# Two key tiles in one visit of the value products, with sixteen homes for the exponentials

## The reference

```python
kv = (mem @ W_kv).reshape(B, Nkv, 2, HEADS, HEAD_DIM)      # mem = ctx_1024, 16 heads of 16
q = (x @ W_q).reshape(B, Nq, HEADS, HEAD_DIM)              # x = layernorm(x)
attn = softmax(einsum('bhqd,bhkd->bhqk', q, k) * SCALE)
out = einsum('bhqk,bhkd->bhqd', attn, v)
x = x + tanh(g_xattn) * (out @ W_proj + b_proj)
# then x = x + tanh(g_ffn) * ffn(layernorm(x)):
# a router picks 2 of 8 experts (silu(g) * u @ w_down, hidden 384) for each token,
# and a shared expert is added for all
```

## Time and profile before

| what | value |
|---|---|
| median of 3 runs | 493.08 us |
| the profiled execution | 493.61 us |
| its span | 491.9 us |
| TensorE, VectorE, ScalarE busy | 97%, 62%, 53% of the span |
| TensorE's granted clock | full up to the last of the 40 slices |

### The profile page before, as it was taken

How to read it: one execution, slowest core, us unless ns; L and a number is a source line. 1 busy time by engine, 2 the same in 40 slices (tenths; PEclk the granted TensorE clock), 3 DMA queues, 4 the chain that set the end, 5 groups by cost and what they waited for, 6 DMA issues and landing times.

```text
span 491.9 us, 7745 instructions
## 1 busy us (share of the span) xinstructions
PE 476.5 (97%) x2783; PEld 286.3 (58%) x2783; DVE 305.9 (62%) x574; ACT 261.0 (53%) x416; POOL 183.9 (37%) x216
## 2 busy tenths in 40 slices
PE   8999999999999999999989999999999999999992
PEld 7665523333233233334446465699799799799992
DVE  3666779999899999996464699533333333333331
ACT  1665277777777777776544400306346346244430
POOL 4810178872231111111000023604547647767332
PEclk9999999999999999999999999999999999999997
DMA  7733408866753565211104001322334525445232
GB/s 246 236 102 105 138 7 228 218 182 183 212 147 87 159 165 163 65 34 55 33 24 149 1 2 43 113 93 46 63 53 65 76 45 87 65 63 78 33 33 32
DMA packets 36741, 48.30 MB, mean 98 GB/s; under 512 B 6240, under 2 KB 29920, under 8 KB 36704
## 3 DMA queue, kind: packets, MB, share of 16 engines
q1 hardware_dynamic: 21536, 26.16, 18.8%
q0 software_dynamic: 7344, 9.84, 13.1%
q10 hardware_dynamic: 7824, 11.81, 7.6%
HBM read 30.16 MB, written 14.29 MB: 90 GB/s over the span
## 4 chain that ended last, share of the span: by engine, by line
PE 94%; DVE 3%; ACT 1%; issue 1%; POOLq 0%; POOL 0%
PE ps L1284 73%; PE ps L1370 13%; PE ps L1646 2%; PE ps L1657 2%; PE ps L1290 1%; PE ps L1679 1%; DVE rows L894 1%; DVE neg_max L929 1%; ACT ctx_region L763 1%; PE ps L1300 1%; PE ps L1362 0%; PE ps L1518 0%; PE ps L1527 0%; POOLq L143 0%; DVE stats L880 0%
## 5 line engine op out<-in xcount | busy, mean ns | idle before, releaser
L763 ACT ACTIVATE ctx_region<-ps 128x512 f32<-128x512 f32 x256 | 140.7, 594 | 47.5 <-PE ps L1284 47.5
L929 DVE TENSOR_REDUCE neg_max<-ps 128x2 f32<-128x1024 f32 x128 | 151.0, 1209 | 21.5 <-PE ps L1284 19.6
L1284 PE MATMUL ps<-unit_region 96*128 96x512 bf16 (+1 forms) x512 | 128.4, 380 | 1.2 <-ACT ctx_region L763 0.7
L1284 PEld LDWEIGHTS ps<-unit_region 96*128 96x128 bf16 (+1 forms) x512 | 45.0, 97 | 101.4 <-ACT ctx_region L763 45.2
L1284 PE MATMUL ps<-unit_region,ctx_region 128*128 128x128 f32 (+1 forms) x824 | 97.4, 274 | 0.0
L1284 PEld LDWEIGHTS ps<-unit_region,ctx_region 128*128 128x128 f32 (+1 forms) x824 | 94.3, 188 | 0.7 <-DVE x_sb L1071 0.3
L655 POOL DMA_INDIRECT out<-unit_region x39 | 61.2, 1570 | 54.2 <-DMA out<-unit_region 31.0
L1284 PE MATMUL ps<-dn_region,unit_region 128*128 (+1 forms) x294 | 70.0, 381 | 0.0
L844 ACT COPY ctx_region<-up_region 128x1536 f32 x33 | 48.5, 1472 | 34.8 <-PE ps L1284 27.2
L1241 DVE TENSOR_TENSOR unit_region<-unit_region,ps 128x384 f32<-128x384 f32 x35 | 19.4, 555 | 71.5 <-ACT unit_region L861 62.6
L1284 PEld LDWEIGHTS ps<-dn_region,unit_region 128*128 128x128 f32 x294 | 53.2, 190 | 8.4 <-issue 2.8
(11 more groups left out here) (200 smaller groups left out, 464.8 us busy)
## 6 DMA issues: line engine op xcount, KB each, us to landing
up_region<-in_w_upT ACTq DMA_DIRECT2D x9, 768.0 KB, 4.5
qk_parts<-up_region SPq DMA_DIRECT2D x24, 192.0 KB, 3.2
unit_region<-qk_parts SPq DMA_DIRECT2D x24, 192.0 KB, 4.1
dn_region<-in_w_downT ACTq DMA_DIRECT2D x9, 384.0 KB, 5.3
unit_region<-up_region SPq DMA_DIRECT2D x48, 64.0 KB, 2.6
unit_region<-qk_parts SPq DMA_DIRECT2D x24, 128.0 KB, 4.1
ctx_region<-in_ctxT SPq DMA_DIRECT2D x4, 512.0 KB, 10.4
x_rows<-rows SPq DMA_DIRECT2D x4, 512.0 KB, 3.9
```

What stands on the lines that cost most here:

```text
L763: nc.scalar.activation(probs[:, k % 8, :], bank(SCORE_HOME[u, k]), ACT.Exp).then_inc(exp_done, 1)
L929: nc.vector.tensor_reduce(neg_max[:, s, 2 * p:2 * p + 2], bank(2 * (p % 2), 2), AX.X, ALU.max, negate=True).then_inc(max_done, 1)
L1284: return nc.tensor.matmul(o_, w, m, start=start, stop=stop)
```

## The change

In units 6 to 13 the visits are made for two key tiles at a time. Key tiles 0 and 1 are visited together behind s9, and key tiles 2 and 3 together behind s1 of the next unit. A visit waits for the exponentials of both of its tiles. Since twice as many exponentials stand at once, those of k = 8 to 15 get eight more homes in xnT, where whole q and k stood until GpSimd had split them (split_done). The waits of ScalarE for free homes are counted anew in visits_ahead.

```diff
@@ -129,6 +129,8 @@
 VALUES = 5
 PAIRS = TOPK * NT
 TABLE_PARTS = 4
+PV_BY_TWO = range(6, 14)
+PROBS = 8
 OUT_ROWS = N + 2 * P
 
 
@@ -154,6 +156,12 @@
         ctx_region = sb("ctx_region", [P, DC * N])
         ctx_sb = ctx_region[:, :].rearrange("p (c n) -> p c n", c=DC)
         probs = ctx_region[:, :].rearrange("p (s n) -> p s n", n=T)
+        probs_beyond = xnT[:, :, :].rearrange("p c n -> p (c n)").rearrange("p (s n) -> p s n", n=T)
+
+        def probs_home(u, k):
+
+            return probs_beyond[:, k - PROBS, :] if u in PV_BY_TWO and k >= PROBS else probs[:, k % PROBS, :]
+
         up_now = ctx_region[:, 0:2 * DC * FFN].rearrange("p (s c f) -> p s c f", s=2, c=DC)
         up_region = sb("up_region", [P, (E + 1) * DC * FFN])
         w_up = up_region[:, :].rearrange("p (e c f) -> p e c f", e=E + 1, c=DC)
@@ -754,13 +762,24 @@
                 act.wait_ge(nmT_ps, u + 1)
                 nc.scalar.copy(nmT[:, :], bank(SCORE_HOME[u - 1, TURNED])[0:HG * TB, 0:P]).then_inc(nmT_sb, 1)
 
+            def visits_ahead(u, kt):
+
+                two, two_ahead = u in PV_BY_TWO, u - 1 in PV_BY_TWO
+                if kt < 2 and two_ahead:
+                    return (u - 1) * TB + 2
+                if kt >= 2 and two:
+                    return u * TB if two_ahead else 0
+                return u * TB + kt - 1
+
             def exp_slot(u, g, first=False, more_max=True):
                 for k in range(TB * HG):
                     kt = k // HG
-                    if k % HG == 0 and not (first and kt < 2):
-                        act.wait_ge(pv_done, u * TB + kt - 1)
+                    if k % HG == 0 and visits_ahead(u, kt) > 0:
+                        act.wait_ge(pv_done, visits_ahead(u, kt))
+                    if u in PV_BY_TWO and k == PROBS:
+                        act.wait_ge(split_done, len(SPLIT_ORDER))
                     act.wait_ge(score_ps, u * TB * HG + k + 1)
-                    nc.scalar.activation(probs[:, k % 8, :], bank(SCORE_HOME[u, k]), ACT.Exp).then_inc(exp_done, 1)
+                    nc.scalar.activation(probs_home(u, k), bank(SCORE_HOME[u, k]), ACT.Exp).then_inc(exp_done, 1)
                     if k == 4 and more_max:
                         copy_max(u + 1)
 
@@ -1363,12 +1382,12 @@
                                     ident[:, :]).then_inc(nmT_ps, 1)
 
             def pv(u, s, kt, first=False):
-                pe.wait_ge(exp_done, u * TB * HG + kt * HG + HG)
+                pe.wait_ge(exp_done, u * TB * HG + (kt | 1 if u in PV_BY_TWO else kt) * HG + HG)
                 if kt == 0 and not first:
                     pe.wait_ge(o_done, u)
                 for h in range(HG):
                     last = nc.tensor.matmul(bank(6)[h * VW:(h + 1) * VW, :], v_home(u // NG)[:, kt, u % NG * HG + h, :],
-                                            probs[:, (kt * HG + h) % 8, :], start=kt == 0, stop=kt == TB - 1,
+                                            probs_home(u, kt * HG + h), start=kt == 0, stop=kt == TB - 1,
                                             skip_group_check=True)
                 last.then_inc(pv_done, 1)
 
@@ -1394,8 +1413,13 @@
                     mm(bank(SCORE_HOME[u, k]), k_unit[0:KROWS + MROWS, s, h, kt * P:(kt + 1) * P],
                        q_unit[0:KROWS + MROWS, s, h, :]).then_inc(score_ps, 1)
                     if k == 1 and not first:
-                        pv(u - 1, (r - 1) % NG, TB - 1)
-                    if kt >= 1 and h == 1:
+                        for last_kt in range(TB - 2 if u - 1 in PV_BY_TWO else TB - 1, TB):
+                            pv(u - 1, (r - 1) % NG, last_kt)
+                    if u in PV_BY_TWO:
+                        if kt == 2 and h == 1:
+                            pv(u, s, 0)
+                            pv(u, s, 1)
+                    elif kt >= 1 and h == 1:
                         pv(u, s, kt - 1, first)
                     if more_max and h == HG - 1:
                         for i in range(2):
```

## The result

The changed kernel takes 503.14 us (median of 4 runs, 502.71 to 503.52), the kernel before 493.07 us in the same comparison: ratio 1.0201, 95% interval [1.0183, 1.0219]. That is 10.1 us slower, where 10.8 us were forecast. The profiled execution took 503.15 us, its span is 501.4 us.

What follows compares the result with a forecast made beforehand. TensorE was taken to bound units 6 to 13. Per unit, - 2 x 0.19 + 0.84 + 0.48 + 0.40 = + 1.34 us; over eight units + 10.8, so 493.08 + 10.8 = 503.9 us, range 496.5 to 507.5.

Steps and rivals of the forecast that it cites:

- What bounds the stretch: Units 6 to 13: TensorE, busy 91.63 of 92 us, bounds them, and its readers have little time to spare.
- the walk: One unit of the new order followed by the old trace's steps: 6.41 + 6.34 = 12.75 us.
- The three waits: TensorE held each unit: s6 for the maxima copy 0.84 us, s15 for an exponential 0.48, m14 for a reduction 0.40.
- 2.00 us, 0.19 less than two apart: Cost of a merged visit on TensorE with 0.45 us between passes; 16 merges save 3.0 us.
- The 0.64 of the other bound: Rival: the step between merged visits costs 0.64 us, nothing saved, 506.9 us; within the 0.85 for all three waits.
- No wait at m6: First half: the second reduction is free at 3.54 us, m6 comes at 3.55, only because s6 has waited.
- Edits at no cost: New homes, ScalarE's waits, weight loads in the merged visit, take_out and SyncE's operand loads add no time.
- Everything behind unit 13 is shifted as a whole: After the changed units, the rest of the kernel only moves later, as TensorE has the chain there too.
- The full gain: Rival: readers keep ahead, TensorE is not held, merges save 3.0 us, 490.1 us; chance 0.05.
- Only the wait of s6: Rival: both second-half waits are covered, + 3.7 us, 496.8 us; chance 0.07.
- The clock: Rival: granted clock falls from 2.4 to 1.2 GHz in these units, up to 85 us more, 578 us; chance 0.02.
- The profile's signs: Units 12.7 to 12.8 us, three waits, passes 0.45 us apart, VectorE idle over 1 us, TensorE busy 87%, clock 1.00.

Runs made afterwards that it cites:

- e2: The changed kernel with only key tiles 0 and 1 visited together, 2 and 3 one at a time behind s13 and s1; 498.4 us, ratio 1.0101.
- e3: The changed kernel with only key tiles 2 and 3 visited together, 0 and 1 one at a time behind s5 and s9; 498.15 us, ratio 1.0102.
- e5: The changed kernel with the copy of the transposed maxima behind the exponential of k = 3, not k = 4, in units 6 to 13; 502.97 us.
- e7: The changed kernel with the copy behind the exponential of k = 3 and reductions over half of the keys in units 6 to 13; 496.78 us.
- e4: The changed kernel with the two visits of each pair pushed apart by one score; 506.87 us, ratio 1.0277.
- e8: The kernel before, with VectorE's reductions over half of the keys in units 6 to 13; 492.72 us against 493.38, ratio 0.9989.
- e1: The changed kernel without its merges, keeping the sixteen homes and ScalarE's new waits; 493.25 us against 492.95, ratio 1.0007.
- e10: The changed kernel with half-key reductions, visits reordered behind s1 and s10, copy behind the exponential of k = 3; 490.11 us, ratio 0.9941.
- e6: The changed kernel with VectorE's reductions over half of the keys in units 6 to 13; 499.02 us, ratio 1.0114.
- e9: The changed kernel reordered, both merges kept: visits behind s0 and m7, copy behind the exponential of k = 3, full reductions; 500.52 us, ratio 1.0151.
- e12: The kernel of e9 with each visit waiting only for its own key tile's exponentials; 495.41 us, ratio 1.0042.
- e11: The kernel of e10 with its order kept but reductions over all keys; 506.04 us, ratio 1.0269.

## Why the prediction was right, point by point

- **What bounds the stretch.** Right. TensorE had no slack there, so every wait and every saving came out nearly one to one: the old unit 11.45 us, the new one 12.73, forecast 12.75 by the walk.
- **The three waits.** Right in place, cause and size. Start to start in the changed kernel, s15 at 166.07 was due at 163.63 + 9 x 0.217 = 165.58, 0.49 us held (0.48 forecast); m14 at 167.12 comes 3.49 us behind s10 (3.48). s6 at 172.63 comes 2.69 us behind s2 at 169.94 (2.68), where 1.84 was due, 0.85 us held (0.84). e2 and e3 show each wait with its half, e5 to e7 which engine causes which.
- **The term that was mis-sized** is "2.00 us, 0.19 less than two apart". The first pass of a visit is 0.45 us, each later one 0.43: 0.31 - 0.22 + 0.45 + 0.43 + 0.43 + 0.55 = 1.95 us, so a merge saves 0.24. e4 measured 0.23. Over 16 merges this is 16 x 0.05 = 0.8 us. The 0.64 of the other bound falls, and with it that rival. The measured 0.43 agrees with what the Trainium skill (TensorEngine Tiling (Array Packing), Tiling Modes, Key Properties) says, that only a change of the tiling mode drains the engine.
- **Where the 10.8 and the 10.1 us part.** The 0.8 us above are near the difference of 0.7, but they are not its account. With them alone the new unit would be 12.65 us, and it is 12.73. Small terms went the other way: m6 is held 0.03 us, the second matmul behind each wait comes 0.01 us later than usual, and the old unit is 11.45 us where its steps give 11.43. That the walk met the unit within 0.02 us is in this part luck. In the traces seven units grow by 1.28 to 1.32 us, 0.3 to 0.4 us less in all than the sum has. The eighth, from the transpose in unit 13 to that in unit 14, goes from 11.31 to 12.30 us, 0.99 more, as the wait of 0.30 us of unit 14 goes (see e8). That gives 10.05 us.
- **No wait at m6 "only because s6 has waited"**: right but for 0.03 us, and e5 is the proof, as the wait appears there.
- **Edits at no cost**: right for the homes and ScalarE's waits (e1). "Everything behind unit 13 is shifted as a whole" is off by the 0.30 us of unit 14. The weight loads stand ahead of the merged visit (166.55 and 166.97 us) and not in it, at no cost: the exponential of k = 15 is done at 3.85, as forecast.
- **Rivals.** The full gain needs fast readers and another order (e10). Only the wait of s6: the second half's waits were both there. The clock: the granted clock stayed 1.00, 2.4 GHz, with TensorE busy 83.50 of 92 us. What the Trainium skill (TensorE: Matmul & The Clock Gate, A second HAM failure mode: psum-queue depth-cycling) tells of short idle times between groups of matmuls did not come about in this kernel.
- **The profile's signs.** All as listed but three. The later passes of a merged visit are 0.43 us apart and not 0.45. VectorE idles 0.75 us ahead of the fifth reduction in units with the transpose back; over 1 us was said, which left that transpose out; the longest such wait, in a unit without it, is 1.4 us. The busy share was 91%, not 87%, as the view counts a matmul for its whole 0.38 us, where the next could start after 0.22: each of three waits a unit hides 0.16 us of it.

One thing is open to the eye. The spans of the profiled executions differ by 9.5 us, less than the medians. In the profile before, unit 6 starts with 0.37 us of waiting that has no releaser in the trace, ahead of its first score:

```profile
128.84 1.40 PE ps L1284 x6
130.25 0.37 issue
130.62 0.59 PE ps L1284 x2
```

By the code this score waits, among others, for the DMA that brings the operands of unit 8. The profile of the changed kernel lacks the wait. Five of the fourteen profiles show one there (before, e2, e6, e7 and e10), the others none, with the merges and without. So it is no part of the change; what makes it come and go stays open.

## What to carry to other kernels

A long piece of work on a saturated engine may be the cover under which its readers empty the buffers; before grouping such pieces to save a switch, walk the order once, from each buffer's release to its next use, and compare with what stands between. Here 0.24 us saved stood against some 0.85 us uncovered, in each half of a unit. Grouping pays only if the buffers last for the longer piece, so give the readers depth or speed first. If a wait goes and the time stays, look for a second engine that came free at the same moment (e5 against e7). And let each part of a group wait only for its own inputs (e9 against e12).

## What the runs showed of the hardware that was not expected

- Of four passes in a row in the same 32-column groups, the step is 0.45 us behind the first pass, which follows a matmul over all 128 columns, and 0.43 us between the later ones.
- TensorE kept its full clock (1.00) with waits of 0.4 to 0.9 us three times in every 12.7 us, over eight units.
- A start-to-start sum over three engines, made from one trace of the old order, gave the new order's unit within 0.02 us (12.75 against 12.73), with small errors that cancel. For other orders of the same work it came within 0.15 us (e10, e11, e12), and failed only where a wait of the code was left out of it (e9).
